# First expert from whole gathered rows turned on TensorE, with the last attention tiles reordered

## The reference, cut to what matters

```python
# B = 4 sequences of S = 1024 tokens, H = 1024 columns, T = 4096 tokens in all
s = softmax(where(mask, -inf, (ctx @ Wq.T + bq) @ (ctx @ Wk.T + bk).T / 16 * layernorm(x)))
x = x + tanh(g_xattn) * s
h = layernorm(x)
w, sel = top_k(softmax(h @ gate_w.T), 8); w = w / sum(w)        # 64 experts, 8 for each token
inp = the first 256 rows of h that chose expert e               # [64, 256, 1024]
o = (silu(inp @ wg[e]) * (inp @ wu[e])) @ wd[e]                 # 384 columns inside
x = x + tanh(g_ffn) * (each token's sum of w * o)
```

## Time and profile before

| | us |
|---|---|
| median of 3 runs | 1843.42 (1843.0 to 1848.21) |
| the profiled execution | 1842.44 |
| its span, first to last instruction | 1840.7 |
| PE busy | 1797.5 (98%) |
| DVE busy | 1450.3 (79%) |
| ACT busy | 1236.2 (67%) |
| POOL busy | 1064.7 (58%) |

### The profile page before, as it was taken

The page is one execution under the profiler, slowest core; times in us unless marked ns, Lnnn a source line. Parts: engine busy times, 40 slices in busy tenths (PEclk is TensorE's granted clock), DMA queues, the critical chain, the costliest instruction groups (busy, mean ns, idle before and its releaser), DMA issues.

```text
span 1840.7 us, 37183 instructions
## 1 busy us (share of the span) xinstructions
PE 1797.5 (98%) x13149; PEld 1316.9 (72%) x13149; DVE 1450.3 (79%) x2523; ACT 1236.2 (67%) x1806; POOL 1064.7 (58%) x817
## 2 busy tenths in 40 slices
PE   9999986999999999999999999999999999999997
PEld 4666655777777777777777777777777777777775
DVE  5999998777777777777777777777777777777772
ACT  6999986566666666666666666666666666666662
POOL 1000002776667666666666666677667766666651
PEclk9999997999999999999999999999999999999999
DMA  8677753799989999999999999999999999999982
GB/s 257 217 247 267 240 209 147 267 324 300 301 283 313 300 298 299 300 299 299 302 302 304 304 305 306 303 305 306 307 302 301 297 300 299 299 299 298 299 285 46
DMA packets 93849, 516.98 MB, mean 281 GB/s; under 512 B 17136, under 2 KB 19696, under 8 KB 69872
## 3 DMA queue, kind: packets, MB, share of 16 engines
q1 hardware_dynamic: 47056, 357.19, 49.3%
q0 software_dynamic: 43008, 151.04, 34.7%
q10 hardware_dynamic: 3744, 8.26, 1.6%
HBM read 409.21 MB, written 107.22 MB: 281 GB/s over the span
## 4 chain that ended last, share of the span: by engine, by line
PE 89%; DVE 5%; issue 2%; DMA 2%; ACT 1%; SPq 0%; POOL 0%; POOLq 0%; DVEq 0%; ACTq 0%
PE ps_gu L531 54%; PE ps_d L540 27%; PE ps_s L412 4%; PE ps_l L432 2%; PE ps_j L401 2%; DMA xb<-in_x 1%; DVE zb L898 1%; DVE zb L870 1%; PE ps_t L424 1%; DMA xg<-h_rows,g_idx 1%; DVE at L932 1%; PE ps_w L447 0%; DVE at L940 0%; ACT hT L645 0%; DVE hrow L960 0%
## 5 line engine op out<-in xcount | busy, mean ns | idle before, releaser
L1304 POOL DMA_INDIRECT xg<-h_rows,g_idx x504 | 724.5, 1437 | 187.9 <-issue 132.4
L531 PE MATMUL ps_gu<-xT,split_g 128*128 128x256 bf16 x4608 | 534.4, 273 | 0.7 <-DVE xT L1186 0.7
L531 PE MATMUL ps_gu<-xT,split_u 128*128 128x256 bf16 x4608 | 534.4, 273 | 0.0
L540 PE MATMUL ps_d<-split_d,act 128*128 128x512 bf16 x2304 | 507.9, 379 | 0.4 <-DVE act L1138 0.4
L531 PEld LDWEIGHTS ps_gu<-xT,split_g 128*128 128x128 bf16 x4608 | 450.8, 98 | 66.5 <-issue 0.9
L531 PEld LDWEIGHTS ps_gu<-xT,split_u 128*128 128x128 bf16 x4608 | 450.9, 98 | 52.2
L540 PEld LDWEIGHTS ps_d<-split_d,act 128*128 128x128 bf16 x2304 | 225.3, 98 | 259.1 <-DVE act L1138 1.2
L783 ACT ACTIVATE ob<-ps_d,wcol 128x512 f32<-128x512 f32 x256 | 173.1, 688 | 338.3 <-PE ps_d L540 338.3
L1324 POOL DMA_INDIRECT out<-ob,s_idx x128 | 205.4, 1604 | 294.2 <-ACT ob L783 202.5
L1146 DVE STREAM_TRANSPOSE xt<-xg 128x512 f32<-128x512 f32 x252 | 163.9, 689 | 151.2 <-DMA xg<-h_rows,g_idx 151.2
L1128 DVE TENSOR_TENSOR split_d<-raw_d,split_d 128x1536 bf16<-128x1536 f32 x128 | 219.3, 1753 | 73.1 <-ACT split_d L755 73.1
(11 more groups left out here) (116 smaller groups left out, 1402.3 us busy)
## 6 DMA issues: line engine op xcount, KB each, us to landing
raw_d<-in_wd SPq DMA_DIRECT2D x63, 1536.0 KB
raw_g<-in_wg SPq DMA_DIRECT2D x62, 1536.0 KB
raw_u<-in_wu SPq DMA_DIRECT2D x62, 1536.0 KB, 16.0
h_rows<-hrow SPq DMA_DIRECT2D x34, 640.0 KB, 3.4
xb<-in_x SPq DMA_DIRECT2D x32, 512.0 KB, 4.4
out<-xb SPq DMA_DIRECT2D x32, 512.0 KB, 3.2
xg<-h_rows,g_idx POOLq DMA_INDIRECT x512, 3.3
ctx_sb<-in_ctxT SPq DMA_DIRECT2D x8, 512.0 KB, 6.0
```

The lines of the kernel that those rows point to most:

```text
L531: mm = pe.matmul(ps_gu[m][:, t, :], w[:, wi, k, m * P:(m + 1) * P], xT[u][:, k, xi, :], start=(k == 0 and (wi, xi) == (0, 0)), stop=(k == ...
L540: mm = pe.matmul(ps_d[n][:], act[u][:, ai, m, half * P:(half + 1) * P], split_d[:, wi, m, c * NH:(c + 1) * NH], start=(m == 0 and (wi, ai) ...
L1304: p.indirect_dma_start(out=xg[u][:, g, :], out_offset=None, in_=h_rows, in_offset=bass.IndirectOffsetOnAxis(ap=g_idx[u][:, g:g + 1].bitcas ...
```

## The change

It has four parts. First, five `xb` buffers in place of four, and one `ctx` buffer in place of two, whose halves are loaded separately; the weight pieces of the start go out in other tiles, those of expert 0's gate and up as two DMAs a piece, in the row order in which a stored token row has its columns. Second, in the last seven passes of PE's loop 14 idle matmuls stand ahead of `logits`; on DVE each tile's `q_` step moves from the end of one tile to behind `scaled_scores` of the next. Third, the tail's steps are reordered, its idle matmuls are 24, 8, 8, 8 instead of 0, 12, 8, 24, the last tile's row is stored in two parts (1024 columns as soon as it is normalised, the shares behind routing), and ACT's table for silu is loaded ahead of `attention_done`. Fourth, DVE writes the integer `table` straight from PSUM; POOL gathers expert 0's 256 rows with two indirect DMAs of 128 rows of 5120 bytes; PE turns them in sixteen 128 x 128 transposes into `ps_d`; ACT and DVE make the high and low parts in four pieces of 512 columns from PSUM; PE starts the gate product of block 0 when the first piece is there, and does the gate products of all three blocks before the up products.

```diff
@@ -91,12 +91,14 @@
+    NX = 5
+    h_lines = h_rows.rearrange("(t q) c -> t (q c)", q=QS)
...
-        ctx_sb = [sb(f"ctx_sb{i}", [P, CC, S], F32, a_mem) for i in range(2)]
+        ctx_sb = sb("ctx_sb", [P, CC, S], F32, a_mem)
         qk = [sb(f"qk{i}", [P, 2, CC, S], F32, a_mem) for i in range(2)]
-        xb = [sb(f"xb{i}", [P, H], F32, a_mem) for i in range(4)]
+        xb = [sb(f"xb{i}", [P, H], F32, a_mem) for i in range(NX)]
...
-        WEIGHT_TILES = [g for g in range(3, N) if g not in (TB, TB + 1)][0:5 * PARTS]
+        WEIGHT_TILES = [g for g in range(3, N) if g % 4 != 1][0:5 * PARTS]
...
+            for i in range(NX):
+                eng.wait_ge(x1_stored[i], 16 * len(range(i, N, NX)))
             for i in range(4):
-                eng.wait_ge(x1_stored[i], 16 * N // 4)
-                eng.wait_ge(h_stored[i], 16 * N // 4)
+                eng.wait_ge(h_stored[i], 16 * N // 4 + (16 if i == (N - 1) % 4 else 0))
         @block.sync
         def _(sp):
-            def load_ctx(b):
-                for n in range(2):
-                    cols = slice(n * NH, (n + 1) * NH)
-                    sp.dma_start(ctx_sb[b % 2][:, :, cols], ctxT[b, :, :, cols]).then_inc(ctx_loaded[b % 2][n], 16)
+            def load_ctx(b, n):
+                cols = slice(n * NH, (n + 1) * NH)
+                if b:
+                    sp.wait_ge(proj_done, 8 * b - 4 + 4 * n)
+                sp.dma_start(ctx_sb[:, :, cols], ctxT[b, :, :, cols]).then_inc(ctx_loaded[n], 16)
             def load_x(g):
-                sp.dma_start(xb[g % 4][:], x[g * P:(g + 1) * P, :]).then_inc(x_loaded[g % 4], 16)
+                sp.dma_start(xb[g % NX][:], x[g * P:(g + 1) * P, :]).then_inc(x_loaded[g % NX], 16)
...
             load_x(2)
             load_x(3)
-            load_ctx(1)
+            load_x(4)
             sp.wait_ge(consts_made, CONSTS)
             for half in range(2):
                 r = slice(T + half * P, T + (half + 1) * P)
                 sp.dma_start(h_whole[r], hrow[3][:]).then_inc(rows_cleared, 16)
                 sp.dma_start(out[r, :].rearrange("t (q c) -> t q c", q=QS), hrow[3][:, :, 0:QH]).then_inc(rows_cleared, 16)
+            load_ctx(1, 0)
             for g in range(N):
                 b, j = g // TB, g % TB
-                if 1 <= g < N - 3:
-
-                    sp.wait_ge(x1_stored[(g - 1) % 4], 16 * ((g - 1) // 4 + 1))
+                if 1 <= g <= N - NX:
+
+                    sp.wait_ge(x1_stored[(g - 1) % NX], 16 * ((g - 1) // NX + 1))
                     sp.wait_ge(h_done, g)
-                    load_x(g + 3)
+                    load_x(g - 1 + NX)
                 sp.wait_ge(x1_ready, g + 1)
-                sp.dma_start(out[g * P:(g + 1) * P, :], xb[g % 4][:]).then_inc(x1_stored[g % 4], 16)
+                sp.dma_start(out[g * P:(g + 1) * P, :], xb[g % NX][:]).then_inc(x1_stored[g % NX], 16)
                 if g >= 3:
                     store_h(g - 3)
-                if j == 0 and b < B - 2:
-                    sp.wait_ge(proj_done, 8 * (b + 1))
-                    load_ctx(b + 2)
+                if j == 1 and b < B - 1:
+                    load_ctx(b + 1, 1)
+                if j == 5 and b < B - 2:
+                    load_ctx(b + 2, 0)
                 if j == 0 and b < B - 1:
                     sp.wait_ge(kpm_used, b + 1)
                     load_kpm(b + 1)
-            for g in range(N - 3, N):
-                store_h(g)
+            sp.wait_ge(h_done, N)
+            sp.dma_start(h_whole[(N - 1) * P:N * P, :, 0:QH], hrow[(N - 1) % 4][:, :, 0:QH]).then_inc(h_stored[(N - 1) % 4], 16)
+            store_h(N - 3)
+            store_h(N - 2)
+            sp.wait_ge(routed, N)
+            sp.dma_start(h_whole[(N - 1) * P:N * P, :, QH:QW], hrow[(N - 1) % 4][:, :, QH:QW]).then_inc(h_stored[(N - 1) % 4], 16)
...
             for g in range(N - 1):
                 if g >= 2:
                     turn_h(g - 1)
                 if g + TB < N:
                     project(g // TB + 1, g % TB)
+                else:
+                    pe.wait_ge(proj_out, 8 * B)
+                    idle_turns(14)
                 if g >= 1:
                     logits(g - 1)
                 if g + 2 < N:
                     scores(g + 2)
-            def idle_turns(n):
-
-                for _ in range(n):
-                    pe.matmul(ps_j[:, 0:P], ones[:], ones[:], start=True, stop=True)
-
-            pe.wait_ge(proj_out, 8 * B)
+            idle_turns(24)
             positions(N - 3)
             turn_h(N - 2)
             places(N - 5)
-            idle_turns(12)
+            idle_turns(8)
             logits(N - 2)
             turn_h(N - 1)
             places(N - 4)
@@ -502,7 +517,7 @@
             counts()
             idle_turns(8)
             places(N - 2)
-            idle_turns(24)
+            idle_turns(8)
             places(N - 1)
...
+            def half_gate_up(e, u, m, t, first=False):
+                w = (split_g, split_u)[t][u]
+                if m == 0:
+                    pe.wait_ge((g_low, u_low)[t], 2 * e + 2)
+                for k in range(KH):
+                    if m == 0 and t == 0 and k % 2 == 0:
+                        if first:
+                            pe.wait_ge(first_low, k // 2 + 1)
+                        else:
+                            pe.wait_ge(xT_out, 4 * e + k // 2 - 3)
+                    for wi, xi in PAIRS:
+                        mm = pe.matmul(ps_gu[m][:, t, :], w[:, wi, k, m * P:(m + 1) * P], xT[u][:, k, xi, :],
+                                       start=(k == 0 and (wi, xi) == (0, 0)),
+                                       stop=(k == KH - 1 and (wi, xi) == (1, 0)))
+                return mm
+
+            def gate_up(e, u, m):
+                pe.wait_ge(act_ready, MI * e - MI + m + 1)
+                half_gate_up(e, u, m, 0)
+                half_gate_up(e, u, m, 1).then_inc(gu_done, 1)
...
+            def first_turns():
+
+                for half in range(2):
+                    pe.wait_ge(first_rows[half], 16)
+                    for k in range(KH):
+                        mm = pe.transpose(ps_d[k // 2][:, k % 2 * CAP + half * P:k % 2 * CAP + (half + 1) * P],
+                                          xg[0][:, QS * half + k // 2, k % 2 * P:(k % 2 + 1) * P], ident[:])
+                        if half:
+                            mm.then_inc(first_turned, 1)
+
+            def first_expert():
+
+                for m in range(MI):
+                    half_gate_up(0, 0, m, 0, True)
+                for m in range(MI):
+                    half_gate_up(0, 0, m, 1, True).then_inc(gu_done, 1)
+                down(0, 0, True)
             attention_done(pe)
             marks = ident[:].bitcast(BF16)
-            for g in range(4, NG):
-                pe.wait_ge(first_turned, g)
-                for _ in range(10):
-                    pe.matmul(ps_d[3][:, 0:2 * P], marks[:, 0:P], marks, start=True, stop=True)
-            expert(0, 0, True)
+            for _ in range(24):
+                pe.matmul(ps_gu[2][:].rearrange("p t c -> p (t c)")[:, 0:2 * P], marks[:, 0:P], marks, start=True, stop=True)
+            first_turns()
+            first_expert()
...
-                if name < 4:
+                if name < 2:
+                    raw, src, loaded = ((raw_g[0], wg, g_loaded[0]), (raw_u[0], wu, u_loaded[0]))[name]
+                    rows = slice(part * 32, (part + 1) * 32)
+                    for n in range(2):
+                        s.dma_start(raw[:, 2 * part + n], src[0, rows, 4 * n:4 * n + 4].rearrange("i k c -> k i c")
+                                    ).then_inc(loaded, 16)
+                elif name < 4:
...
             expert_weights(N - 1)
+            row_shares(N - 1)
             place_tokens(N - 2)
-            row_shares(N - 1)
+            s.activation(silu_warm[:], ident[:, 0:1], ACT.Silu).then_inc(silu_table, 1)
...
-            def first_high_part(g):
-                ts = slice(g * 32, (g + 1) * 32)
-                s.wait_ge(first_turned, g + 1)
-                s.activation(xT[0][:, :, 0, ts], xt[:, :, ts], ACT.Copy).then_inc(first_high, 1)
+            def first_high_part(n):
+                s.wait_ge(first_turned, 2 * n + 2)
+                s.activation(xT[0][:, 2 * n:2 * n + 2, 0], ps_d[n][:].rearrange("p (k c) -> p k c", k=2), ACT.Copy
+                             ).then_inc(first_high, 1)
...
             def first_expert():
-                s.activation(ob[1][:, 0, 0:1], ident[:, 0:1], ACT.Silu).then_inc(silu_table, 1)
                 for part in range(2):
                     gate_high(0, 0, part, True)
-                for part in range(2):
-                    up_high(0, 0, part, True)
-                for g in range(5):
-                    first_high_part(g)
+                for n in range(4):
+                    first_high_part(n)
+                s.activation(wcol[0][:], xg[0][:, 0::QS, QH], ACT.Copy).then_inc(wcol_ready, QS)
+                up_high(0, 0, 0, True)
```

(68 more changed lines are left out.)

66 lines of the change are left out of this document (26 added, 40 removed).

## The result

The changed kernel takes 1835.45 us (median of 5 runs, 1833.68 to 1838.28) against 1843.42 us. The ratio is 0.9956, with a 95% interval of 0.9945 to 0.9968: faster by 8.0 us or 0.44%, where 11.8 us were forecast. The profiled execution took 1835.45 us with a span of 1833.6, against 1842.44 and 1840.7: 7.1 us of span.

The account below looks back on a forecast made before the run. TensorE in the experts' products bounds the kernel, so only expert 0's start and duration can move. Terms -2.2, -2.8, -0.4, -0.8, -9.4, +3.8 sum to -11.8 us from 1842.44: 1830.6 us; range 1827 to 1837, 8 in 10.

Parts of the forecast that it names:

- The step that failed: Tiles: moved weight pieces are the same bytes, extra issues lie beside a 1 us activation, nothing delays SP's loads; no cost.
- The x buffers: Tiles 10 and 11: the fifth buffer removes ACT's wait for x, gaining 2.2 us, bounds 0 to 2.6.
- The fourteen idle matmuls: Tiles 28 and 29: they keep the clock at 2.4 GHz, gaining 2.8 us, or 0 if it falls.
- `q_` and the tail: `q_` behind the scores gains 0.4 us; fewer idle matmuls and the reordering in the tail gain 0.8 us.
- Table to gates: Table's first write to expert 0's first gate matmul: 9.4 us instead of 18.85, so 9.4 us earlier.
- Expert 0, (b): Expert 0's `down` waits for DVE's `activate`: 1.1 us, then 0.3 us for block 2.
- the full-clock case: Rival: clock stays at 2.4 GHz over the gathers, DVE delays `down` 1.7 + 0.3, expert 0 25.5 us; 1829.8; chance 0.15.
- Expert 0, (a): Expert 0's gate products start at 1.2 GHz and stay there for 4.7 us, losing 2.35 us.
- The rival with 0.15: Clock stays at 2.4 GHz over expert 0's gathers, so the low-clock loss is gone; 1829.8 us; chance 0.15.
- Landing at its upper bound: Rival: gathers land 3.3 us later and the shares' store costs 1.4 us before expert 0; 1836.3 us; chance 0.12.
- Issue by bytes: Rival: POOL's gather issue time goes by bytes, 5.5 us an issue, 8.2 us later; 1839.8 us; chance 0.05.
- A gap on DVE per tile: Rival: the moved `q_` step opens a DVE gap in 28 tiles; at 0.6 us each 1848.4 us; chance 0.04.

Follow-up runs that it names:

- e2: Kernel before, with only its first eight weight pieces loaded as the changed kernel does (two DMAs of four row groups each): 1849.45 us, ratio 1.0032.
- e4: Changed kernel with DVE's `activate` of blocks 1 and 2 of expert 0 ahead of expert 1's two `up_low` pieces: 1837.33 us, ratio 0.9962.
- e9: Changed kernel with the last tiles' order and idle matmuls of before (12, 8, 8 and 24): 1837.55 us, ratio 0.9966.
- e11: Changed kernel with expert 0's gate and up pieces cut to 32 partitions outermost, still two transfers each, and four x buffers: 1834.22 us, ratio 0.9941.
- e7: Changed kernel without the 24 idle matmuls behind the table: 1836.92 us, ratio 0.9965.

## Why the forecast was right and wrong, step by step

*The step that failed* in the tiles is the sentence on the weight pieces under the five x buffers, that they "are as many bytes in other tiles, and eight more issues on ACT lie beside an activation of 1 us", and with it "nothing takes its place on SP". Bytes and issues were right. What I left out is how many engines carry a transfer: four, so that a piece of 384 KB takes some 4 us at 104 GB/s, 0.25 of the DMA share, and the row stores issued meanwhile land late, after 6.9 us at the median instead of 3.7. ACT waits 8.0 us in six tiles for them. Shown twice: the pieces alone cost 5.9 us in the kernel before, and widening them gains 4.8 us in the tiles of the changed one. The stretch missed its forecast by 5.0 us; that is more than the 3.8 us by which the whole missed.

*The x buffers*: the number is right, 2.1 us measured against 2.2 where the stores are not held up, but in part by luck. The wait at tile 10 is gone with four buffers, too (16.54 us for the two tiles), and the fifth buffer pays by four other, shorter waits that the forecast did not name.

*The fourteen idle matmuls*: right. The clock stayed, and the two tiles came back to 16.37 us. In all eleven executions of a changed kernel the tiles 24 to 29 take 8.2 us at most; in both kernels without the idle matmuls (before and e2) two tiles of 9.4 to 9.7 us stand among the last eight. No run parts the idle matmuls from the moved `q_` step.

*`q_` and the tail*: -3.4 us against -4.0 over the stretch from tile 27's store, of which 2.8 are the clock's. Undoing the tail's order cost 0.8 us in one execution, the forecast's 0.8, but the spread between executions of the same tail is 1.3 us, so this term is suggested and not shown. Forecast and trace seem to differ if one measures from tile 31's store (17.06 against 16.29 before), because tile 31's store itself moved by 1.35 us. The 0.6 us that are missing go with the clock at 1.2 GHz from 302.5 to 305.9, after PE had stood 2.27 us: with more idle matmuls in the gaps the clock stayed up and the same stretch was 45.23. That part is suggested by one execution, not shown by a timed difference.

*Table to gates*: mis-sized by 2.0 us, 11.38 against 9.4. The second gather issues at +3.4 instead of +2.7, as POOL's hand-over behind the table is 0.8 us longer than assumed (the registers explain 0.1 of it); the first issue itself was right, 1.30 us against 1.37. The second half of the rows lands 5.8 us after its issue and not 4.7, 1.1 more: a window over it has 410 GB/s, and the first half is on the way with it. Whether that overlap is the reason is not shown; no run gathers one half alone. The transposes and the hand-over to the gates are 0.2 us more. By the Trainium skill's rule that the forecast weighed (DMA: Bandwidth & Descriptors, Anatomy of one DMA — SWDGE (gpsimd) path) the landing would be 3.5 us, an estimate; no whole-row gather here took less than 5.0.

*Expert 0, (b)*: right in kind, 1.3 us in all, where the full-clock case had 1.7 + 0.3. Reordering DVE's queue took it to nothing, 23.49 us, but expert 1 then gave back 0.2, 0.8 and 1.6 us in the three runs with that order.

*Expert 0, (a)*: wrong in this execution. The clock fell during the gathers, at 312.8, as forecast, but was back at 316.2, before the first gate matmul. The rival with 0.15, in which it never falls, describes the gates rightly and the gathers not. Which case comes is not the same in every execution: of the eight with the change's 24 idle matmuls three (e4, e9, e11) had gates at 1.2 GHz, and expert 0 was 0.65 to 1.7 us longer; without them (e7) it was 1.8, and in the two with 48 the gates had the full clock. So 2.35 us was too much for a mean. The 4.7 us of low clock behind it stand on no row. A reading beside them is off, too: finer windows of the kernel before have the clock back at 322.2, 4.9 us after the idle matmuls had started, not at 322.93 and 5.7.

The errors are +5.0, +0.6, +2.0, -2.5 and -0.4, together 4.7, which takes -11.8 to the 7.1 us of the span. The range held the time because errors of opposite sign met, the tiles and the table's stretch against expert 0; that the result lies within it is in part luck.

*The other rivals.* Landing at its upper bound came in small part: 1.1 us of its 4.7, and the store of the shares, issued at 301.5 and landed 2.3 us later, was in before the table. Issue by bytes is excluded: 1.30 and 1.82 us for four times the bytes, where it had 5.5. A gap on DVE per tile was not seen: tiles 12 to 27 take 125.0 us with the wide pieces, as they did before (124.9).

*Open*: whether transposes count for TensorE's clock. In the changed kernel the clock came back at 316.0 to 316.5, when PE had run nothing but the sixteen transposes since 309.8. Without idle matmuls it ran the same sixteen from 314.89 to 319.06 and the clock stayed low until 323.0. The Trainium skill's statement that they don't (TensorE: Matmul & The Clock Gate, Part 4: PE-mode transpose) fits the second and not the first.

## What to carry to other kernels

When a transfer's pattern changes, look at its outermost dimension in the diff, before bytes and issue counts; a DMA share that stands at a simple fraction (here 0.25) in the windows is the sign, and the victim is another transfer that is issued behind it. A small mend can cost what it saves: more and narrower issues (four of 0.6 us) outran the activation that covered two, and a step moved forward in one expert came back as a wait in the next, so look one stage further before a gain is booked. Where idle matmuls hold the clock, their number is a bet on it: 24 that end early cost nothing, and 48 that began at the low clock made the way to the gates 0.6 us longer. And where executions of one kernel spread by 1 us over a stretch, a gain of 0.8 us in it needs more than one trace.
